# Joined sums of weighed states: VectorE's and TensorE's order at the join moved by one state

## The chip, the core and the metric

The kernel runs on one core of one Trainium2 chip. The metric is the device time in microseconds (us). Five engines work side by side, each with a queue of its own that it takes in order: TensorE (PE, matrix products and transposes), VectorE (DVE), ScalarE (ACT), GpSimd (POOL) and SyncE (SP, which here issues DMAs). They wait for each other by semaphores.

## What is computed

Two transformer-like layers over 2048 tokens of width 512. Layer 0 is a masked linear layer and a SwiGLU block with low-rank parts. Layer 1 is a selective state-space layer followed by a small mixture of experts. The change lies in the state-space layer, whose core is this recurrence over the tokens, for 1024 channels (`D_IN`) and 16 states (`N`):

```python
def step(state, inp):
    dt_t, B_t, C_t, u_t = inp
    dA = jnp.exp(dt_t[..., None] * A)
    state = state * dA + (dt_t * u_t)[..., None] * B_t[:, None, :]
    y = jnp.einsum('bdn,bn->bd', state, C_t)
    return (state, y)
```

So `y` is a sum over the 16 states, each weighed with its column of `C`. Around it stand the input projection, a convolution over four tokens, the projections that give `dt`, `B` and `C`, the gate, the output projection, a router and the experts.

## The kernel before, in words

Layer 1 takes the 2048 tokens in eight chunks of 256 (`NCH`, `CH`). In a chunk `i` the 1024 channels are two groups of 512 (`NDG`), and each group has 16 states: 32 steps `s`, written by hand as 32 slots in a loop of every engine (`iteration`). `st = s % 16` is the state in its group. Chunk `i`'s slots also carry work of the chunk before it (`p`: output projection, router, experts) and of the next one (`n`: input projection `x_tile`, `convolve`, `u`, `wx`, `dt_tile`, gates). The first chunk has no `p`, the last no `n`.

What one state costs, by engine:

- GpSimd makes `dbu` (`db`, L2097), dt times u times B, up to four states ahead of the scan.
- ScalarE writes the exponentials into `ps_a` (`exps`, L1757), in two halves, four instructions a state. There is one `ps_a`, so the half of state `s` waits for the scan of the same half of state `s - 1`. Between the halves it keeps the last column of the state before (`keep_state`, L1777).
- VectorE scans: `h` from `ps_a` and `dbu`, in two halves (`scans`, L2273). `h` is a ring of four states.
- The sum over the states is made with tokens on the partitions, so TensorE turns `h` (a transpose, eight passes, four for each of two halves `t` of the tokens) into the PSUM banks `ps_h`.

The states of a group are summed in two ways. For states 0 to 3 (`KC = 4`) GpSimd weighs `h` with `C` (`weigh_h`, L2131), and TensorE adds them up inside PSUM while it turns them (`add_h`, L1487; `init_acc`, L1475, puts in the term with D). After state 3 ScalarE copies that sum to `acc` in two halves: that is the join (`join_acc`, L1949, in the slot with `st == JOIN_AT`, 5, behind the exponentials of state 6 in its queue and ahead of those of state 7). For states 4 to 15 TensorE turns `h` unweighed (`turn_h`, L1502) and VectorE adds it to `acc` with its weight from `c_cur` (`add_state`, L2289, two instructions, one for each `t`).

`ps_h` has one bank for each `t`. So `turn_h` of state `s` waits, half by half, until state `s - 1` is added (for state 4: until its half is joined), and until state `s` is scanned. `add_state` waits for the turn of its half. The scan of state `s` waits for the turn of state `s - 4`, for `dbu` and for its half of `ps_a`.

The order at the join, before. VectorE: scan 5, scan 6, add 4, scan 7, add 5, add 6, scan 8, add 7, scan 9, add 8, and from there on one scan and one addition a slot. TensorE in the first group of a middle chunk: `add_h` of state 3, turn 4, a quarter of the output projection (q 5, L1526), turn 5, q 6, turn 6, `x_tile` 0, turn 7, q 7, `x_tile` 1, turn 8, `convolve` 0, `x_tile` 2, turn 9. In the second group: turn 4, `turn_tsb`, turn 5, the first part of the experts, turn 6, `dt_tile` 0 and 1, turn 7, turn 8, `dt_tile` 2 and 3, a second part of the experts, turn 9.

Other lines that the steps below touch: `make_u` (VectorE, L2303) reads the bank that `x_tile` and `convolve` of a tile wrote; `x_tile(m)` waits for `u` of tile `m - 3`, which had the same bank. `dt_add` (GpSimd, L2177) needs ScalarE's logarithm (`dt_log`, L1882) of the next chunk.

Of the kernel before, what the change touches and what calls it, by code (L numbers as in the profile page):

```python
# [42 lines left out]
NS = 16  # L43
# [40 lines left out]
JOIN_AT = 5  # L84
# [1026 lines left out]
def layer_1(nc, A, x2_dram, bt_dram, out, W, c, sb, ps, sems):  # L1111
# [229 lines left out]
    def _(pe):  # L1341
# [260 lines left out]
        def iteration(i, p, n, first, second):  # L1602
            for s in range(STEPS):
                st = s % NS
                if st == JOIN_AT + 1:
                    turn_h(i, s - 2)
                elif st == JOIN_AT + 2:
                    turn_h(i, s - 1)
                elif st > JOIN_AT + 2:
                    turn_h(i, s)  # L1610
                if first:
                    for m in GB_FIRST.get(s, ()):
# [24 lines left out]
                if s == FIRST_X:  # L1637
                    if n is not None:
                        x_tile(n, 0, False)
                    turn_h(i, s)  # L1640
                if p is not None and s:
                    for q in WO_AT.get(s, ()):
                        out_projection(p, q)
                        if q == 5:
                            turn_h(i, s - 1)
                if p is not None and s == RA_AT:
                    pe.wait_ge(S["t4_lo"], p * TT + TT)
                    router(p)
# [37 lines left out]
                    add_h(i, s - st + ADD_AT[st], first)  # L1686
                if st == 3:
                    init_acc(i, s // NS)
                if st == JOIN_AT + 1 and (p is None or s > NS):
                    turn_h(i, s - 1)  # L1690
                if p is not None and n is not None and s == NS + JOIN_AT + 1:
                    experts(p, 0)
                if st == JOIN_AT + 2 and s != FIRST_X:
                    turn_h(i, s)

        for m in range(3):
# [560 lines left out]
    def _(dve):  # L2257
# [147 lines left out]
        def iteration(i, p, n, first, second):  # L2405
            for s in range(STEPS):
                scans(i, s, first)
                st = s % NS
                if s == 0 and not first:
                    make_sg(i, 2)  # L2410
                if n is not None:
                    for m in at_slot(XT_AT, s, 4):
                        make_u(n, m)
                if s == JOIN_AT + 1:
                    dve.wait_ge(S["c_done"], i + 1)
                if st == JOIN_AT + 2:
                    add_state(i, s - 2)
                elif (st == 0 or st > JOIN_AT + 2) and not (first and s == 0):
                    add_state(i if s else i - 1, (s - 1) % STEPS)
                if p is not None:  # L2420
                    for m in at_slot(YB_AT, s):
                        make_y(p, m)
                if first and s == 2:
                    make_sg_first(2)
                    make_sg_first(3)
                if s == (3 if first else 2):
                    make_sg(i, 4)
                if p is not None and s == 4:
                    add_out_projection(p, 0)
                if s == 4:  # L2430
                    make_sg(i, 6)
                if p is not None and s == 8:
                    add_out_projection(p, 1)
                for m in at_slot(YA_AT, s):
                    make_y(i, m)
                if n is not None and s == WX_AT + 4:
                    make_sg(n, 0)
                if n is not None and s == WX_AT + 3:
                    mean_squares(n)
                if n is not None and s == WX_AT + 5:  # L2440
                    rms_apply(n)
                if p is not None and s == RA_AT + 3:
                    choose(p)
                if st == JOIN_AT + 1:
                    add_state(i, s - 2)
                if st == JOIN_AT + 2:
                    add_state(i, s - 1)

        nc.vector.memset(hist[:], 0.0).then_inc(S["begun"], 1)
# [99 lines left out]
```

## Time and profile before

| | us |
|---|---|
| time, median of 3 runs | 1513.37 (1512.45 to 1514.31) |
| time of the profiled execution | 1512.44 |
| its span, first to last instruction | 1510.3 |
| PE busy, share of the span | 1349.8, 89% |
| DVE busy | 1213.1, 80% |
| POOL busy | 1028.2, 68% |
| ACT busy | 952.1, 63% |
| L2273, the scans, x512 | 595.8, 1205 ns each |
| L2289, the additions, x384 | 267.9, 737 ns each |
| L1502, the turns, x1536 passes | 226.4, idle before them 65.3, of it 60.0 for L2289 |

Layer 1's scans begin at 530.5 us and end at 1476 us; layer 0 and the preparation of layer 1 lie before. In the rows below a time is the start of an instruction or of a run of like ones (x says how many), the next number how long it took, and brackets hold the idle time of the engine before it with what ended that. Matmuls overlap, so the distance from one start to the next is their cost, not the time in the row. PEclk is the share of full speed (2.4 GHz) that TensorE was granted.

### The profile page before, as it was taken

What the parts mean: (1) busy time and instruction counts of PE and PEld (TensorE: products, weight loads), DVE (VectorE), ACT (ScalarE), POOL (GpSimd) and SP (SyncE); (2) the same over time, 40 slices, a digit from 0 to 9 for tenths busy, and PEclk for the clock granted to TensorE, in tenths of its full rate; (3) what the DMA queues carried; (4) which work ended last, traced back from release to release, by engine and by line L of the source; (5) the groups of instructions that cost most, each with busy time, mean ns of one, the idle gap of its engine ahead of it and who ended that gap; (6) DMA issues with size and microseconds to landing.
All of it is one profiled execution on the core that took longest, in us unless ns stands there. A gap on an engine that the chain in (4) does not pass through costs nothing.

```text
span 1510.3 us, 25293 instructions
## 1 busy us (share of the span) xinstructions
PE 1349.8 (89%) x8817; PEld 1006.2 (67%) x8817; DVE 1213.1 (80%) x1643; ACT 952.1 (63%) x2617; POOL 1028.2 (68%) x697
## 2 busy tenths in 40 slices
PE   6899999999999959699899899899899999988677
PEld 5566677768776748568668667667766766855543
DVE  5794674556443469999999999999999999999994
ACT  3432343233321577788888897798798888886761
POOL 0353242313212398998998999899899899899870
PEclk9799999999999979899999999999999999999689
DMA  9531222101100200100110110020030020020001
GB/s 331 195 112 37 91 79 84 56 29 36 36 29 15 87 18 1 57 29 15 57 42 1 57 57 1 31 83 1 15 99 1 15 86 14 1 71 29 1 1 42
DMA packets 32388, 77.16 MB, mean 51 GB/s; under 512 B 3667, under 2 KB 4723, under 8 KB 31750
## 3 DMA queue, kind: packets, MB, share of 16 engines
q1 hardware_dynamic: 32262, 75.55, 15.1%
q8 instruction: 70, 1.15, 0.3%
q14 instruction: 56, 0.46, 0.1%
HBM read 66.99 MB, written 8.55 MB: 50 GB/s over the span
## 4 chain that ended last, share of the span: by engine, by line
PE 31%; POOL 13%; DVE 12%; ACT 6%; issue 5%; DVEq 0%; ACTq 0%; POOLq 0%
PE ps_h L1502 10%; DVE h L2273 7%; POOL h L2131 7%; POOL dbu L2097 6%; PE ps_m L1466 4%; DVE acc L2289 3%; ACT ps_a L1757 2%; PE ps_o L1526 2%; PE ps_m L165 2%; PE ps_s L1466 2%; PE ps_m L166 2%; PE ps_m L167 2%; PE ps_m L1426 2%; ACT ab L1889 1%; PE ps_s L165 1%
## 5 line engine op out<-in xcount | busy, mean ns | idle before, releaser
L2273 DVE TENSOR_TENSOR_SCAN h<-ps_a,dbu 128x512 f32<-128x512 f32 x512 | 595.8, 1205 | 21.3 <-ACT ps_a L1757 7.1
L2097 POOL TENSOR_TENSOR dbu<-dtu,b_all 128x1020 f32<-128x1020 f32 x256 | 598.3, 2358 | 14.4 <-DVE h L2273 13.9
L1757 ACT ACTIVATE ps_a<-dt,a_neg 128x256 f32<-128x256 f32 (+1 forms) x1024 | 442.9, 466 | 67.7 <-DVE h L2273 66.6
L1502 PE MATMUL ps_h<-ident,h 128*128 128x128 f32 x1536 | 226.4, 290 | 65.3 <-DVE acc L2289 60.0
L2289 DVE SCALAR_TENSOR_TENSOR acc<-ps_h,c_cur,acc 128x512 f32<-128x512 f32 x384 | 267.9, 737 | 16.9 <-PE ps_h L1502 16.3
L1502 PEld LDWEIGHTS ps_h<-ident,h 128*128 128x128 f32 x1536 | 183.1, 149 | 123.0 <-DVE h L2273 82.4
L724 POOL TENSOR_TENSOR hid_l<-hid,hid_h 128x256 f16<-128x256 f32 (+1 forms) x88 | 77.4, 883 | 155.0 <-ACT hid_h L610 154.8
L2131 POOL TENSOR_TENSOR h<-h,c_all 128x1024 f32<-128x1024 f32 x64 | 151.1, 2362 | 19.2 <-ACT carry L1777 19.2
L602 ACT ACTIVATE sil<-ps_gu 128x256 f32<-128x256 f32 (+1 forms) x88 | 33.9, 385 | 180.6 <-PE ps_gu L167 180.6
L165 PE MATMUL ps_m<-h_h,wi_h 128*128 128x256 f16 x432 | 119.4, 276 | 2.6 <-PEq L155 2.4
L166 PE MATMUL ps_m<-h_l,wi_h 128*128 128x256 f16 x432 | 119.2, 276 | 0.0
L167 PE MATMUL ps_m<-h_h,wi_l 128*128 128x256 f16 x432 | 119.2, 276 | 0.0
L1526 PE MATMUL ps_o<-wo,y 128*128 128x512 f32 x224 | 107.6, 603 | 7.7 <-DVE x L2391 7.7
L1487 PE MATMUL ps_h<-ident,h 128*128 128x128 f32 x512 | 70.4, 283 | 36.9 <-POOL h L2131 36.8
L165 PE MATMUL ps_gu<-h_h,g_h 128*128 128x256 f16 (+1 forms) x352 | 96.6, 274 | 3.8 <-DVE u_l L1016 2.9
L1487 PEld LDWEIGHTS ps_h<-ident,h 128*128 128x128 f32 x512 | 59.9, 145 | 56.0 <-POOL h L2131 43.7
L167 PE MATMUL ps_gu<-h_h,g_l 128*128 128x256 f16 (+1 forms) x352 | 96.5, 274 | 0.0
L166 PE MATMUL ps_gu<-h_l,g_h 128*128 128x256 f16 (+1 forms) x352 | 96.5, 274 | 0.0
L165 PE MATMUL ps_gu<-h_h,u_h 128*128 128x256 f16 (+1 forms) x352 | 96.1, 273 | 0.0
L166 PE MATMUL ps_gu<-h_l,u_h 128*128 128x256 f16 (+1 forms) x352 | 96.1, 273 | 0.0
L167 PE MATMUL ps_gu<-h_h,u_l 128*128 128x256 f16 (+1 forms) x352 | 96.1, 273 | 0.0
L732 POOL COPY x<-x 128x1024 f32<-128x1024 f32 x8 | 8.3, 1037 | 120.5 <-issue 120.5
(406 smaller groups left out, 2876.8 us busy)
## 6 DMA issues: line engine op xcount, KB each, us to landing
b_all<-bt_scratch SPq DMA_DIRECT2D x32, 512.0 KB, 3.9
wm<-in_wmod SPq DMA_DIRECT2D x7, 1024.0 KB, 5.2
wo<-in_wmod SPq DMA_DIRECT2D x5, 1024.0 KB, 8.6
xa<-in_x SPq DMA_DIRECT2D x8, 512.0 KB, 4.5
stage<-in_W_in SPq DMA_DIRECT2D x4, 1024.0 KB
x_scratch<-x SPq DMA_DIRECT2D x8, 512.0 KB, 3.1
c_all<-bt_scratch SPq DMA_DIRECT2D x8, 512.0 KB, 6.0
x<-x_scratch SPq DMA_DIRECT2D x8, 512.0 KB, 3.6
```

Of the source, the lines that this page charges most:

```text
L165: pe.matmul(out, lh, rh, start=(first and k == 0), stop=False)
L166: pe.matmul(out, lh, rl, start=False, stop=False)
L167: mm = pe.matmul(out, ll, rh, start=False, stop=(last and k == n - 1))
L1466: pe.matmul(x_bank(m, first), diag_t[:, m, tap], xw[:, m % 2, tap:tap + CH], start=(tap == 0), stop=False)
L1487: tr = pe.matmul(ps_h[:, t, j * P:(j + 1) * P], h[:, s % RING, j, t * P:(t + 1) * P], W["ident"][:], is_transpose=True, start=(begin and j ...
L1502: tr = pe.transpose(ps_h[:, t, j * P:(j + 1) * P], h[:, s % RING, j, t * P:(t + 1) * P], W["ident"][:])
L1526: mm = pe.matmul(ps_o[:], y[:, k, tok], W["wo"][:, k], start=(k == 0), stop=(k == KI - 1))
L1757: ex = nc.scalar.activation(ps_a[:, j, j % 2:], dt[:, m, j % 2:], ACT.Exp, scale=a_neg[:, m, st:st + 1])
L2097: nc.gpsimd.tensor_tensor(dbu[:, s % AHEAD, :, 1:], dtu[:, :, 1:], b_all[:, st, 1:].unsqueeze(1).to_broadcast([P, DG, CH - 1]), ALU.mult). ...
L2131: nc.gpsimd.tensor_tensor(h[:, s % RING], h[:, s % RING], c_all[:, s % NS, :].unsqueeze(1).to_broadcast([P, DG, CH]), ALU.mult).then_inc(S ...
L2273: nc.vector.tensor_tensor_scan(h[:, s % RING, two].rearrange("p j t -> p (j t)"), ps_a[:, two].rearrange("p j t -> p (j t)"), dbu[:, s % A ...
L2289: op = nc.vector.scalar_tensor_tensor(part, ps_h[:, t], c_t, part, ALU.mult, ALU.add)
```

## The change

VectorE adds state 4 one slot later, after the scan of state 7. To come level again it adds two states in the slots of states 7 and 8 (4 and 5, 6 and 7) where before it added one in the slot of state 6 and two in that of state 7. TensorE's turns move along: turn 5 goes to the head of slot 7, turn 6 behind `x_tile` 0 or to the end of slot 7, turn 7 to the head of slot 8 and turn 8 to its end. The scans, `dbu`, the exponentials, the join and all DMAs stay where they are.

The order after. VectorE: scan 6, scan 7, add 4, add 5, scan 8, add 6, add 7, scan 9, add 8. TensorE in the first group: turn 4, q 5, q 6, turn 5, `x_tile` 0, turn 6, q 7, `x_tile` 1, turn 7, `convolve` 0, `x_tile` 2, turn 8, turn 9. In the second group: turn 4, `turn_tsb`, the first part of the experts, turn 5, `dt_tile` 0 and 1, turn 6, turn 7, `dt_tile` 2 and 3, the second part of the experts, turn 8, turn 9.

```diff
@@ TensorE, iteration
                 if st == JOIN_AT + 1:
                     turn_h(i, s - 2)
                 elif st == JOIN_AT + 2:
+                    turn_h(i, s - 2)
+                elif st == JOIN_AT + 3:
                     turn_h(i, s - 1)
-                elif st > JOIN_AT + 2:
+                elif st > JOIN_AT + 3:
                     turn_h(i, s)
...
                 if s == FIRST_X:
                     if n is not None:
                         x_tile(n, 0, False)
-                    turn_h(i, s)
+                    turn_h(i, s - 1)
                 if p is not None and s:
                     for q in WO_AT.get(s, ()):
                         out_projection(p, q)
-                        if q == 5:
-                            turn_h(i, s - 1)
...
-                if st == JOIN_AT + 1 and (p is None or s > NS):
-                    turn_h(i, s - 1)
                 if p is not None and n is not None and s == NS + JOIN_AT + 1:
                     experts(p, 0)
                 if st == JOIN_AT + 2 and s != FIRST_X:
+                    turn_h(i, s - 1)
+                if st == JOIN_AT + 3:
                     turn_h(i, s)
@@ VectorE, iteration
                 if st == JOIN_AT + 2:
+                    add_state(i, s - 3)
+                elif st == JOIN_AT + 3:
                     add_state(i, s - 2)
-                elif (st == 0 or st > JOIN_AT + 2) and not (first and s == 0):
+                elif (st == 0 or st > JOIN_AT + 3) and not (first and s == 0):
                     add_state(i if s else i - 1, (s - 1) % STEPS)
...
-                if st == JOIN_AT + 1:
+                if st == JOIN_AT + 2:
                     add_state(i, s - 2)
-                if st == JOIN_AT + 2:
+                if st == JOIN_AT + 3:
                     add_state(i, s - 1)
```

## Rows read from the trace of the kernel before

**Rows 1.** Chain of waits: page's shares by engine, then two pieces.
```profile
PE 31%; POOL 13%; DVE 12%; ACT 6%; issue 5%; DVEq 0%; ACTq 0%; POOLq 0%
...
902.27 2.41 DVE h L2273 x2
...
1020.36 2.41 DVE h L2273 x2
```

**Rows 2.** Busy by stretch: us, PE, PEld, DVE, ACT, POOL, PEclk, DMA share, GB/s.
```profile
911.06:953.36 42.30, 42.30 (x286) 35.27 (x286) 40.74 (x52) 34.76 (x111) 35.69 (x23) 1.00 0.04 14
953.36:973.66 20.30, 16.75 (x140) 13.70 (x139) 19.34 (x32) 16.05 (x48) 20.13 (x11) 1.00 0.00 1
863.89:867.39 3.50, 3.50 (x20) 2.13 (x20) 3.50 (x5) 2.91 (x9) 3.34 (x8) 1.00 0.81 260
982.06:985.56 3.50, 3.50 (x14) 2.50 (x13) 3.50 (x5) 2.90 (x9) 3.34 (x8) 0.54 0.82 261
```

**Rows 3.** Timeline of DVE at the first join and after it.
```profile
911.77 1.41 DVE L2289 SCALAR_TENSOR_TENSOR acc<-ps_h,c_cur,acc 128x512 f32<-128x512 f32 x2 [1.06 <-PE ps_h L1502]
...
916.89 1.41 DVE L2289 SCALAR_TENSOR_TENSOR acc<-ps_h,c_cur,acc 128x512 f32<-128x512 f32 x2 [0.17 <-PE ps_h L1502]
...
928.35 0.42 DVE L2303 SCALAR_TENSOR_TENSOR u<-th,ps_m 128x256 f32<-128x256 f32 x1
```

**Rows 4.** Timeline of PE at the first join and after it.
```profile
911.04 1.06 PE L1502 MATMUL ps_h<-ident,h 128*128 128x128 f32 x8 [0.40 <-ACT acc L1949]
911.94 1.88 PE L1526 MATMUL ps_o<-wo,y 128*128 128x512 f32 x4
913.66 1.04 PE L1502 MATMUL ps_h<-ident,h 128*128 128x128 f32 x8
...
926.51 1.04 PE L1502 MATMUL ps_h<-ident,h 128*128 128x128 f32 x8
927.38 1.89 PE L1466 MATMUL ps_m<-xw,diag_t 128*128 128x256 f32 x8
...
929.22 0.27 PE L165 MATMUL ps_m<-h_h,wi_h 128*128 128x256 f16 x1
...
930.53 1.04 PE L1502 MATMUL ps_h<-ident,h 128*128 128x128 f32 x8
```

**Rows 5.** Timeline of ACT at the first join.
```profile
910.29 1.09 ACT L1949 ACTIVATE acc<-ps_h 128x512 f32<-128x512 f32 x2 [1.13 <-PE ps_h L1487]
...
911.74 0.89 ACT L1757 ACTIVATE ps_a<-dt,a_neg 128x256 f32<-128x256 f32 x2
```

**Rows 6.** Timeline of DVE at the second join and after it.
```profile
973.64 2.34 DVE L2273 TENSOR_TENSOR_SCAN h<-ps_a,dbu 128x512 f32<-128x512 f32 x2 [0.51 <-POOL dbu L2097]
...
981.01 1.38 DVE L2289 SCALAR_TENSOR_TENSOR acc<-ps_h,c_cur,acc 128x512 f32<-128x512 f32 x2
982.31 2.33 DVE L2273 TENSOR_TENSOR_SCAN h<-ps_a,dbu 128x512 f32<-128x512 f32 x2
```

**Rows 7.** Timeline of PE after the second join.
```profile
981.88 1.68 PE L1502 MATMUL ps_h<-ident,h 128*128 128x128 f32 x8 [2.15 <-DVE acc L2289]
983.35 1.91 PE L1426 MATMUL ps_m<-tsb,w_dt 128*128 128x256 f32 x4
...
986.92 1.04 PE L1502 MATMUL ps_h<-ident,h 128*128 128x128 f32 x8
```

**Rows 8.** Timelines of ACT and of POOL, later in the second group.
```profile
990.34 1.05 ACT L1882 ACTIVATE ab<-ab 128x1024 f32<-128x1024 f32 x1
...
984.61 6.98 POOL L2097 TENSOR_TENSOR dbu<-dtu,b_all 128x1020 f32<-128x1020 f32 x3
991.56 2.37 POOL L2177 TENSOR_TENSOR dt<-dt,ab 128x1024 f32<-128x1024 f32 x1
```

**Rows 9.** Timelines of POOL in the first and of DVE in the last chunk.
```profile
636.90 2.36 POOL L2177 TENSOR_TENSOR dt<-dt,ab 128x1024 f32<-128x1024 f32 x1 [3.20 <-ACT ab L1882]
...
1442.70 1.41 DVE L2289 SCALAR_TENSOR_TENSOR acc<-ps_h,c_cur,acc 128x512 f32<-128x512 f32 x2 [2.15 <-PE ps_h L1502]
```

## The prediction

> **What bounds the kernel now.** Layer 1 runs eight chunks of 256 tokens, and from the second to the seventh one repeats the other, so I worked on one chunk and multiplied. I read the chain of waits first: TensorE carries most of it, with GpSimd and VectorE behind; the chain passes the same two scans at 902.27 and at 1020.36, so a chunk takes 118.1 us, and this one (number 3, counted from 0) is the one I worked on [rows 1]. That is an average over stages, so I then took the busy times by stretch [rows 2]. In the 42.3 us from the turn of state 4 to the scan of state 16 TensorE is busy for all 42.30, VectorE for 40.74 and GpSimd for 35.69: TensorE sets the time. I call this stage B. In the 20.3 us after it GpSimd is busy for 20.13; this is stage C, and it ends with GpSimd's `dbu` for state 23. From there to the next chunk's state 3 VectorE is busy nearly without a break; I call it stage D. GpSimd in it has no idle time worth naming either: its row of three `dbu` ends at 991.59 and `dt_add` starts at 991.56, just after ScalarE's logarithm ended at 990.34 + 1.05 = 991.39 [rows 8].
>
> The change touches the joins, at slots 6 to 9 of each group of 16 states: the first lies at the head of stage B, the second at the head of stage D. The question is what it does to TensorE there in B, and to VectorE there in D.
>
> **Part 1: VectorE scans state 7 before it adds state 4.** No instruction is added or removed; each state has two scans (one pair takes 2.24 us from start to next start) and two additions (1.30). Before, VectorE waits 1.06 us for the turn of state 4, adds it at 911.77, and scans state 7 when the two additions are over, at 913.10 [rows 3]. The gap looks as if it could be filled with the scan. But that scan reads `ps_a`, whose exponentials ScalarE writes only after the two copies of the join (`join_acc` stands ahead of `exps(7)` in its queue): the copies run from 910.29, the exponentials of the first half from 911.74 for 0.89 us [rows 5]. So the scan can start near 912.72, only 0.4 us earlier than before, and state 4's addition moves from 911.77 to 912.72 + 2.24 = 914.96.
>
> **Part 2: who waits for that, in stage B.** Two latencies come from the rows: a turn's second half may start 0.87 us after the matching addition started (addition at 981.01, turn at 981.88), and an addition starts 0.73 us after its turn started (911.04, 911.77) [rows 3, 4, 6, 7]. A turn of eight passes takes 0.87 us from start to next start (926.51 to 927.38), a quarter of an output projection 1.72 (911.94 to 913.66), a convolution 1.84 (927.38 to 929.22), an `x_tile` 1.31 (929.22 to 930.53) [rows 4].
> - Turn 5 now stands behind both quarters: TensorE is there at 911.94 + 3.44 = 915.38. Its halves may go at 914.96 + 0.87 = 915.83 and 915.61 + 0.87 = 916.48, so it ends at 916.92 instead of 916.25: 0.67 us lost. The 0.15 that turn 6 lost before (the 0.17 wait of addition 6 [rows 3]) is saved: +0.5.
> - Turns 6, 7 and 8 have tile work between them. Turns 8 and 9 now stand with nothing between: turn 9 needs state 8 added, which needs turn 8. The first half goes 0.70 + 0.87 after turn 8's start, the second 0.65 later, and 0.44 more ends it: 2.66 us for what took 1.74. +0.9.
> - VectorE comes out later than TensorE: by the same steps it scans state 10 from 928.16 to 930.40, and `u` of tile 0, at 928.35 before [rows 3], comes at 930.40 and is done near 930.9. `x_tile(3)` writes over the bank that it reads, and TensorE is there at 930.66: +0.25. The same for the next two tiles costs some 0.15 together.
>
> Stage B: 0.5 + 0.9 + 0.4 = 1.8 us a chunk. TensorE has no idle time in it to take this up, and stage C starts from its end. From both sides: 1.0 if ScalarE lets the scan go earlier and `u` is in time, 2.4 if each wait is 0.1 to 0.2 dearer.
>
> **Part 3: stage D.** Here VectorE is the one without slack. State 23's scan waits for `dbu` until 973.64 [rows 6]. Before, state 20's addition filled the time ahead of that wait; now it stands behind it. So one addition (1.30 us) falls onto the busy stretch. Additions 5 and 7 each wait 0.24 for their turns, the 0.16 wait of addition 6 goes: 1.6 us, and state 25 is scanned near 983.9 instead of 982.31 [rows 6].
>
> Then the moved turn 8: before it was the first thing of its slot, at 981.88. Now it stands behind turn 7, two `dt` tiles and a part of the experts. In chunk 3 TensorE's granted clock is 0.54 there, so half of the 3.5 us or more at 1.2 GHz, in chunk 2 it is 1.00 [rows 2]. At the low clock that work took from 983.35 to turn 9 at 986.92 before, 3.6 us [rows 7]; turn 7 now ends where turn 8 did, so turn 8 starts at 986.92 and addition 8 at 987.65, where VectorE would be ready at 983.87 + 2.24 = 986.11: 1.5 more, 3.1 in all. At full clock turn 8 starts near 985.4 and nobody waits. Chunks 1, 3 and 6 have the low clock there, three of six.
>
> Does it reach the end? GpSimd would have 1.2 us of slack at the weighing of state 1, but at `dt_add` it has 0.1 [rows 8], and ScalarE's logarithm hangs on VectorE's scans through the exponentials ahead of it in its queue. So 1.5 (full clock) or 2.9 (low clock) passes on. Bounds: 0.3 and 3.2.
>
> Of the clock the Trainium skill (TensorE: Matmul & The Clock Gate, Part 1) says that "the default state is throttled, and activity releases the throttle". By that rule the longer waits of TensorE at the head of stage D would give the low clock in all six chunks and not in three; the trace has it at like waits both ways, so I keep three.
>
> **The two ends.** In the first chunk there is no output projection between the turns; by the same steps I take 1.2 for B and 1.5 for D (there GpSimd waits 3.20 us for the logarithm, so all passes on [rows 9]): 2.7. The last chunk has no tiles of a next one. There VectorE waits 2.15 us at the second join [rows 9], and the scan does fill part of it: one addition more behind, 1.30, less some 0.9 gained twice, and waits of 0.2 to 0.3 for turns: 0.8, between -0.8 and 1.6. Semaphores, DMAs and the other queues (SP, GpSimd's order) are not moved.
>
> **The sum.** 6 x 1.8 = 10.8 for B, 3 x 1.5 + 3 x 2.9 = 13.2 for D, 2.7 and 0.8: +27.5 us. The profiled execution took 1512.4 (span 1510.3 and 2.1 around it) and would take 1539.9; the median of the runs is 0.9 above it, so 1540.9.
>
> **The rivals.**
> 1. Stage D's loss is taken up by slack (GpSimd's 1.2 us, ScalarE overtaking): D gives 0.3 a chunk and B stays: 10.8 + 1.8 + 2.7 + 0.8 = 16, so 1529. For it: GpSimd's slack at the weighing. Against: the 0.1 at `dt_add`.
> 2. The low clock in all six chunks, and longer: 3 x 1.4 = 4.2 more and some, 1546. The page's rule above speaks for it.
> 3. Faster: the filled gap counts and the new waits don't. The scan of state 8 comes 0.4 us earlier (917.8 where the additions of state 6, at 916.89, end at 918.2 [rows 3]), twice in each of seven chunks, and some 0.8 twice in the last: 14 x 0.4 + 1.6 = 7, so 1506. This decides if TensorE had slack of over 1.5 us at turn 9 and VectorE more than an addition's worth in D. Against: TensorE busy 42.30 of 42.30.
> 4. The order doesn't matter, since all engines are level at the end of each stage: 1513.
>
> **How the numbers follow.** My forecast has 0.52, rival 1 0.20, rival 2 0.16, rival 3 0.07, rival 4 0.05. A difference of 0.2%, 3 us, is about what a measurement of this kernel can tell. Faster 0.08, same 0.04, slower 0.88. For the range: B between 1.0 and 2.4, D between 0.3 and 3.2, six times, are 8 to 34 us, with the ends 10 to 38; I take 1524 to 1550, which leaves out rivals 3 and 4 and a little on top.
>
> **What would show it.** In the changed profile: scan 7 starts right behind ScalarE's exponentials and not in the 1.06 us gap; TensorE's idle time before turns (waiting for the additions) appears in stage B, at turn 5 and turn 9, where it had none; the period of the middle chunks is 121.5 to 123 instead of 118.2; VectorE waits for turn 8 at the second join where TensorE's clock is low; `dt_add` on GpSimd waits for ScalarE. It is wrong if the period is under 119.5, if turn 9 doesn't wait, or if GpSimd starts the next chunk's weighing on time.

## The result and the profile after

The changed kernel takes 1546.0 us (median of 6 runs, 1540.75 to 1550.43); the kernel before, run beside it, takes 1512.43 (6 runs, 1510.95 to 1514.31). The ratio is 1.0213, 95% interval 1.0195 to 1.0231: slower by 33.6 us, where +27.5 was forecast (1540.9, range 1524 to 1550). The profiled execution is the lowest of the six, 1540.75, with a span of 1538.6. The stages below come from it, so they have to add up to 28.3 us of span, not to 33.6.

First the page of the kernel after: the chain's shares, and the groups of scans, turns and additions.

```profile
PE 25%; POOL 19%; DVE 12%; issue 7%; ACT 6%; DVEq 0%; POOLq 0%; ACTq 0%
...
L2273 DVE TENSOR_TENSOR_SCAN h<-ps_a,dbu 128x512 f32<-128x512 f32 x512 | 596.4, 1207 | 50.3 <-ACT carry L1777 21.9
...
L1502 PE MATMUL ps_h<-ident,h 128*128 128x128 f32 x1536 | 230.7, 293 | 85.4 <-DVE acc L2289 79.7
L2289 DVE SCALAR_TENSOR_TENSOR acc<-ps_h,c_cur,acc 128x512 f32<-128x512 f32 x384 | 268.7, 740 | 18.0 <-PE ps_h L1502 17.3
```

The work is the same (596.4 us of scans for 595.8, 268.7 of additions for 267.9). What grew is idle time: TensorE waits 79.7 us for additions before its turns, where it waited 60.0. The chain has lost TensorE (31% to 25%) and won GpSimd (13% to 19%), which by itself tells neither where nor why.

So I cut each chunk into stages, at instructions close to the prediction's bounds. Stage B runs from the start of the first join (`acc`, L1949; the prediction began 0.75 us later, at turn 4) to GpSimd's weighing of state 16, C from there to the scan of state 23, D from there to `dt_add` (the prediction let it run on to the next chunk's state 3), and the rest of the chunk is the remainder. From the starts in the timelines, in us:

| chunk | B before | B after | D before | D after | period before | period after |
|---|---|---|---|---|---|---|
| 1 | 42.97 | 44.61 | 17.82 | 20.49 | 118.40 | 122.30 |
| 2 | 42.97 | 44.61 | 17.87 | 20.63 | 118.17 | 122.47 |
| 3 | 42.98 | 44.61 | 17.92 | 20.12 | 118.13 | 121.95 |
| 4 | 42.97 | 44.61 | 17.81 | 19.39 | 118.17 | 121.24 |
| 5 | 42.97 | 44.61 | 17.94 | 20.55 | 118.17 | 122.39 |
| 6 | 42.97 | 44.61 | 17.83 | 20.66 | 118.20 | 122.87 |

C and the remainder are the same within 0.4. The six periods grew by 24.0 us, the first chunk by 3.6 (B 2.0, D 1.6), the last by 1.3, what follows its last addition by 1.6, and what lies ahead of the first chunk's join took 2.2 less: 28.3.

**Stage B.** VectorE at the first join of chunk 3 of the kernel after (start, duration, engine, line; in brackets the idle time before):

```profile
922.39 2.34 DVE L2273 TENSOR_TENSOR_SCAN h<-ps_a,dbu 128x512 f32<-128x512 f32 x2 [1.76 <-ACT carry L1777]
924.65 1.39 DVE L2289 SCALAR_TENSOR_TENSOR acc<-ps_h,c_cur,acc 128x512 f32<-128x512 f32 x2
926.19 1.41 DVE L2289 SCALAR_TENSOR_TENSOR acc<-ps_h,c_cur,acc 128x512 f32<-128x512 f32 x2 [0.15 <-PE ps_h L1502]
...
932.43 1.41 DVE L2289 SCALAR_TENSOR_TENSOR acc<-ps_h,c_cur,acc 128x512 f32<-128x512 f32 x2 [0.68 <-PE ps_h L1502]
933.76 2.33 DVE L2273 TENSOR_TENSOR_SCAN h<-ps_a,dbu 128x512 f32<-128x512 f32 x2
936.46 1.41 DVE L2289 SCALAR_TENSOR_TENSOR acc<-ps_h,c_cur,acc 128x512 f32<-128x512 f32 x2 [0.37 <-PE ps_h L1502]
937.78 2.33 DVE L2273 TENSOR_TENSOR_SCAN h<-ps_a,dbu 128x512 f32<-128x512 f32 x2
940.03 0.40 DVE L2303 SCALAR_TENSOR_TENSOR u<-th,ps_m 128x256 f32<-128x256 f32 x1
```

and ScalarE ahead of the scan of state 7:

```profile
919.93 1.09 ACT L1949 ACTIVATE acc<-ps_h 128x512 f32<-128x512 f32 x2 [0.84 <-PE ps_h L1487]
...
921.38 0.89 ACT L1757 ACTIVATE ps_a<-dt,a_neg 128x256 f32<-128x256 f32 x2
```

The gap of 1.06 us [rows 3] isn't filled but has grown: the scan now waits 1.76 us, until 922.39, just behind the exponentials of its first half (921.38 + 0.89 = 922.27), as in [rows 5]. (The trace puts this wait down to `carry`, L1777, the one that came last by the profile.) TensorE in the same stretch (the group x8 is a turn; L165 here is the first product of `x_tile` 3):

```profile
920.67 1.06 PE L1502 MATMUL ps_h<-ident,h 128*128 128x128 f32 x8 [0.40 <-DVE h L2273]
921.58 3.60 PE L1526 MATMUL ps_o<-wo,y 128*128 128x512 f32 x8
925.52 1.23 PE L1502 MATMUL ps_h<-ident,h 128*128 128x128 f32 x8 [0.35 <-DVE acc L2289]
...
935.82 1.04 PE L1502 MATMUL ps_h<-ident,h 128*128 128x128 f32 x8
937.35 1.22 PE L1502 MATMUL ps_h<-ident,h 128*128 128x128 f32 x8 [0.50 <-DVE acc L2289]
938.41 1.89 PE L1466 MATMUL ps_m<-xw,diag_t 128*128 128x256 f32 x8
940.14 0.27 PE L1467 MATMUL ps_m<-sel,rows 128*128 128x256 f16 x1
940.48 0.28 PE L165 MATMUL ps_m<-h_h,wi_h 128*128 128x256 f16 x1
```

From turn 4 to turn 10 TensorE took 911.04 to 930.53 = 19.49 us before [rows 4], and 920.67 to 941.80 = 21.13 now. Those 1.64 us are all of what B lost, and they lie at three places. From turn 4 to the end of turn 6, without `x_tile` 0, 6.23 us became 6.78 (turn 5 waits and runs slowly): 0.55. Turns 8 and 9, which took 0.87 each, now take 938.41 - 935.82 = 2.59 together for 1.74: 0.85. `x_tile` 3 starts 0.34 behind the instruction before it, where 0.11 is the rule [rows 4]: 0.23.

**Stage D.** VectorE, TensorE and GpSimd at the second join of chunk 3:

```profile
984.91 2.34 DVE L2273 TENSOR_TENSOR_SCAN h<-ps_a,dbu 128x512 f32<-128x512 f32 x2 [1.90 <-POOL dbu L2097]
987.16 1.39 DVE L2289 SCALAR_TENSOR_TENSOR acc<-ps_h,c_cur,acc 128x512 f32<-128x512 f32 x2
989.16 1.60 DVE L2289 SCALAR_TENSOR_TENSOR acc<-ps_h,c_cur,acc 128x512 f32<-128x512 f32 x2 [0.61 <-PE ps_h L1502]
```

```profile
988.04 1.94 PE L1502 MATMUL ps_h<-ident,h 128*128 128x128 f32 x8 [2.98 <-DVE acc L2289]
989.77 1.91 PE L1426 MATMUL ps_m<-tsb,w_dt 128*128 128x256 f32 x4
991.48 1.92 PE L1502 MATMUL ps_h<-ident,h 128*128 128x128 f32 x8
```

```profile
995.88 6.99 POOL L2097 TENSOR_TENSOR dbu<-dtu,b_all 128x1020 f32<-128x1020 f32 x3
1005.03 2.36 POOL L2177 TENSOR_TENSOR dt<-dt,ab 128x1024 f32<-128x1024 f32 x1 [2.16 <-ACT ab L1882]
```

The wait for `dbu` is 1.90 us for 0.51 [rows 6]: nothing stands ahead of it now, and state 20 is added behind it. GpSimd, which had no gap at `dt_add` [rows 8], waits 2.16 us there for ScalarE's logarithm. Turns 5 and 6 take 1.94 and 1.92 us here, for 1.22 and 1.04 in chunk 2: that is the granted clock. The busy times by stretch, PEclk behind the five busy times; the stretches start 2.2 us and 8.2 us behind the scan of state 23, chunks 2, 3 and 4:

```profile
864.65:870.65 6.00, 2.96 (x20) 2.42 (x20) 5.84 (x9) 5.41 (x17) 5.77 (x7) 1.00 0.29 102
870.65:876.15 5.50, 5.46 (x24) 3.78 (x25) 4.30 (x5) 2.94 (x9) 5.34 (x9) 0.69 0.50 182
987.11:993.11 6.00, 5.07 (x20) 4.51 (x20) 5.29 (x8) 4.87 (x15) 5.76 (x7) 0.50 0.29 112
993.11:998.61 5.50, 4.75 (x29) 3.19 (x27) 5.27 (x7) 3.26 (x10) 5.34 (x9) 0.92 0.48 172
1109.05:1115.05 6.00, 2.96 (x20) 2.42 (x20) 5.84 (x9) 5.41 (x17) 5.77 (x7) 1.00 0.37 104
1115.05:1120.55 5.50, 4.82 (x30) 3.49 (x31) 5.35 (x7) 3.34 (x10) 5.34 (x9) 1.00 0.61 177
```

Chunk 4 has the full clock throughout and the shortest D, 19.39. Chunk 3 has 0.50 at turns 5 and 6 (D 20.12); chunks 1, 2, 5 and 6 have 0.69 to 0.70 in the later stretch, ahead of turn 8 (D 20.49 to 20.66). There VectorE waits for turn 8, in chunk 2:

```profile
876.34 1.41 DVE L2289 SCALAR_TENSOR_TENSOR acc<-ps_h,c_cur,acc 128x512 f32<-128x512 f32 x2 [0.93 <-PE ps_h L1502]
```

So D lost 6 x 1.58 = 9.5 us without the clock (chunk 4: 19.39 - 17.81), less 0.3 for the spread of before, and 5.5 us over 19.39 in five chunks.

### The profile page after: what moved, and what is told of

It reads as the page before. It is cut to its first block, busy times and chain, and to the rows that moved or that the text cites. A ratio compares the mean times of both kernels' runs of the same rounds, so it can differ in the third digit from the quotient of the medians.

```text
span 1538.6 us, 25293 instructions
## 1 busy us (share of the span) xinstructions
PE 1357.0 (88%) x8817; PEld 1004.0 (65%) x8817; DVE 1213.8 (79%) x1643; ACT 953.7 (62%) x2617; POOL 1027.3 (67%) x697
## 4 chain that ended last, share of the span: by engine, by line
PE 25%; POOL 19%; DVE 12%; issue 7%; ACT 6%; DVEq 0%; POOLq 0%; ACTq 0%
POOL dbu L2097 10%; PE ps_h L1502 8%; POOL h L2131 8%; DVE h L2273 7%; PE ps_m L1466 3%; DVE acc L2289 3%; ACT ps_a L1757 2%; PE ps_s L1466 2%; PE ps_m L165 2%; PE ps_m L166 2%; PE ps_m L167 2%; PE ps_o L1526 1%; PE ps_m L1426 1%; POOL dtu L2203 1%; POOL rms L2169 1%
## 5 line engine op out<-in xcount | busy, mean ns | idle before, releaser
L2273 DVE TENSOR_TENSOR_SCAN h<-ps_a,dbu 128x512 f32<-128x512 f32 x512 | 596.4, 1207 | 50.3 <-ACT carry L1777 21.9
L1502 PE MATMUL ps_h<-ident,h 128*128 128x128 f32 x1536 | 230.7, 293 | 85.4 <-DVE acc L2289 79.7
L2289 DVE SCALAR_TENSOR_TENSOR acc<-ps_h,c_cur,acc 128x512 f32<-128x512 f32 x384 | 268.7, 740 | 18.0 <-PE ps_h L1502 17.3
L165 PE MATMUL ps_m<-h_h,wi_h 128*128 128x256 f16 x432 | 119.6, 277 | 3.1 <-PEq L155 2.4
L1487 PE MATMUL ps_h<-ident,h 128*128 128x128 f32 x512 | 69.3, 280 | 36.1 <-POOL h L2131 36.1
L165 PE MATMUL ps_gu<-h_h,g_h 128*128 128x256 f16 (+1 forms) x352 | 96.0, 273 | 1.8 <-DVE u_l L1016 1.2
L165 PE MATMUL ps_gu<-h_h,u_h 128*128 128x256 f16 (+1 forms) x352 | 95.9, 273 | 0.0
```

The costliest lines, as they stand in the source:

```text
L165: pe.matmul(out, lh, rh, start=(first and k == 0), stop=False)
L1487: tr = pe.matmul(ps_h[:, t, j * P:(j + 1) * P], h[:, s % RING, j, t * P:(t + 1) * P], W["ident"][:], is_transpose=True, start=(begin and j ...
L1502: tr = pe.transpose(ps_h[:, t, j * P:(j + 1) * P], h[:, s % RING, j, t * P:(t + 1) * P], W["ident"][:])
L2273: nc.vector.tensor_tensor_scan(h[:, s % RING, two].rearrange("p j t -> p (j t)"), ps_a[:, two].rearrange("p j t -> p (j t)"), dbu[:, s % A ...
L2289: op = nc.vector.scalar_tensor_tensor(part, ps_h[:, t], c_t, part, ALU.mult, ALU.add)
```

## The experiments

My theory: B and D each lose by themselves, B by the late turns 5 and 9 and late `u`, D by the addition that fell behind the wait for `dbu`, with the low clock on top. A ratio is to the kernel before, measured beside it, with its 95% interval. B and D are those of the middle chunks of the profiled execution.

**One join alone.** Both sides, TensorE and VectorE, of the change in one group of states only. The first join (in the second one `late = 0`; VectorE's first place, against the kernel before, the other places are left out):

```diff
-                if st == JOIN_AT + 2:
+                late = 1 if s // NS == 0 else 0
+                if late and st == JOIN_AT + 2:
+                    add_state(i, s - 3)
+                elif st == JOIN_AT + 2 + late:
                     add_state(i, s - 2)
```

> The change at the first join of each chunk (slots 6 to 9) alone; the second join keeps its old order. My theory: the two joins lose time separately. Stage B (first join to the weighing of state 16) is 1.6 us longer in each middle chunk, as in the changed kernel's trace (44.61 for 42.97), stage D (scan of state 23 to dt_add) stays at 17.9. Sum with the first chunk about +12 us, a time near 1524.5. Rival: stage D is longer because VectorE comes out of stage B late; then D lengthens here too, and the time is 1535 or more.

Measured: 1526.01 (4 runs), 1.0089 [1.0072, 1.0106]; B 44.61, D 17.8 to 18.0. As expected: B loses its 1.63 alone, and D nothing.

The second join (`late = 1 if s // NS == 1 else 0`):

> The change at the second join (slots 22 to 25) alone. My theory: stage B stays at 42.97, stage D goes from 17.9 to 19.5 where TensorE's clock is full and to 20.5 where it is low near turns 5 to 8; sum +17 to +21 us, a time near 1531, with a wider spread between executions than before (which had 3.4 us). Rival (slack takes up the loss): D at most 0.5 longer, a time under 1518.

Measured: 1522.75 (4 runs), 1.0071 [1.0054, 1.0088]; B 42.98 to 42.99, D 20.74 in chunk 1 and 19.39 in the five others. The place is right, but the size is under what I expected, because the low clock came ahead of turn 8 in one chunk of six. The busy times by stretch for chunks 1 and 3 (PEclk 0.85 and 1.00):

```profile
739.81:751.31 11.50, 8.43 (x43) 6.01 (x44) 10.14 (x13) 8.47 (x25) 11.10 (x15) 0.85 0.49 139
980.38:991.88 11.50, 7.80 (x51) 5.93 (x51) 11.19 (x15) 8.76 (x26) 11.10 (x15) 1.00 0.49 141
```

The two together are 13.6 + 10.3 = 23.9 us of the 33.6. I find no third cause in the order of the work: B and D have the same values as in the whole change wherever the clock is full. Of the 9.7 us that are left, the traces show 4.15 as the low clock behind the second join (5.5 us in five chunks of the whole change, 1.35 in one here). Another 5.3 is how far the median of the whole change lies above its profiled execution, and no trace shows what that is.

**One engine alone.** VectorE's new order with TensorE's old one (against the kernel after; the first of TensorE's places, the others go back in the same way):

```diff
@@ TensorE, iteration
                 if st == JOIN_AT + 1:
                     turn_h(i, s - 2)
                 elif st == JOIN_AT + 2:
-                    turn_h(i, s - 2)
-                elif st == JOIN_AT + 3:
                     turn_h(i, s - 1)
```

> VectorE's new order with TensorE's old one. My theory: what costs in stage D is VectorE's own addition behind the wait for dbu (+1.57, the same in all chunks, since turn 8 stands ahead of the dt tiles again and the clock can't reach VectorE), so D is 19.4 to 19.5 in every chunk. In stage B turn 5 waits ahead of q 6 and turn 8 for an addition behind the out projection's: B about +3. Sum near +31 us, a time near 1543. Rival (TensorE's moved turns are what costs): B and D near the old values, a time under 1520.

Measured: 1555.52 (4 runs), 1.029 [1.0273, 1.0307]; B 46.4 to 47.8, D 20.0 to 21.0. That is slower than I said, in both stages. The old turn 5 waits for the late addition of state 4 (2.07 us at the first join, 4.29 at the second) and holds up what follows it, q 6 at the first join; VectorE then waits for that projection:

```profile
938.41 0.69 DVE L2391 SCALAR_TENSOR_TENSOR x<-ps_o,x 128x512 f32<-128x512 f32 x1 [2.93 <-PE ps_o L1526]
```

I had said that the clock couldn't reach VectorE at the second join in this order. It did: the granted clock was low in all six chunks around or behind the wait for turn 5, and D is 20.0 to 20.2 in four chunks and 21.0 in the two where it stayed low for more than 8 us behind the scan of state 23. There is no chunk with the full clock, so this run doesn't show what the order alone costs in D. B is 46.4 in three chunks and 47.6 to 47.8 in the three where the clock was low at the first join too.

TensorE's new order with VectorE's old one (against the kernel after, the first of two places):

```diff
@@ VectorE, iteration
-                if st == JOIN_AT + 2:
-                    add_state(i, s - 3)
-                elif st == JOIN_AT + 3:
+                if st == JOIN_AT + 2:
                     add_state(i, s - 2)
```

> TensorE's new order with VectorE's old one. My theory: turn 9 right behind turn 8 costs 0.9 and the wait of x_tile 3 for u 0.3: B +1.3. In stage D turn 6 now stands behind dt tiles 0 and 1, which wait for ScalarE's copy until about 3.8 us after the scan of state 23, so addition 6 comes 1.5 late: D +1.6, more where the clock is low. Sum +18 to +24, a time near 1534. Rival (VectorE's order alone is what costs): a time within 3 us of before.

Measured: 1533.26 (4 runs), 1.0133 [1.0116, 1.015]; B 44.52 to 44.53, D 19.38 to 19.40 in all six. As expected, with B 0.25 us a chunk above what I said. Late turns cost nearly as much in B as the whole change, late additions alone more: that turns move along with the additions is the cheaper way to do it, not a cure. With VectorE's old order, state 20 is added ahead of the wait for `dbu`, and D still is 19.4, since the addition of state 22 now waits 1.72 us for turn 6. That turn starts at 987.94, behind `dt` tiles 0 and 1, for which TensorE waited 2.75 us for ScalarE, as I had expected:

```profile
983.22 2.34 DVE L2273 TENSOR_TENSOR_SCAN h<-ps_a,dbu 128x512 f32<-128x512 f32 x2 [0.51 <-POOL dbu L2097]
988.58 1.41 DVE L2289 SCALAR_TENSOR_TENSOR acc<-ps_h,c_cur,acc 128x512 f32<-128x512 f32 x2 [1.72 <-PE ps_h L1502]
```

```profile
986.97 1.13 PE L1426 MATMUL ps_m<-tsb,w_dt 128*128 128x256 f32 x4 [2.75 <-ACT tsb L1904]
987.94 1.04 PE L1502 MATMUL ps_h<-ident,h 128*128 128x128 f32 x8
```

So D's 1.58 us come from VectorE's moved addition in the whole change and from TensorE's moved turn 6 here. Taking back VectorE's order alone doesn't win them back.

**Is turn 9 a term of its own?** In the kernel after, turn 8 goes ahead of `x_tile` 2 at the first join, so that a tile lies between turns 8 and 9:

```diff
+                if s == JOIN_AT + 3:
+                    turn_h(i, s)
                 if n is not None:
                     for m in XT_AT.get(s, ()):
...
-                if st == JOIN_AT + 3:
+                if s == NS + JOIN_AT + 3:
                     turn_h(i, s)
```

> The whole change, but at the first join turn 8 stands ahead of x_tile 2 and no longer right ahead of turn 9. My theory: the wait between turns 8 and 9 (0.9 by my sum, 1.5 start to start for 0.87 of work) is then covered by the tile, and addition 8 and u follow earlier; a wait of about 0.3 stays. Stage B of the middle chunks 43.6 to 43.8 for 44.61, stage D as in the changed kernel, a time 5 to 7 us below it, near 1540. Rival (the loss in B is turn 5's wait and VectorE's lateness, whatever stands between 8 and 9): B within 0.2 of 44.61.

Measured: 1543.54 (4 runs), 1.0195 [1.0167, 1.0223]; B 44.64. The rival holds: no gain. TensorE at the same place (turn 9, the convolution, the instruction ahead of `x_tile` 3, its first product):

```profile
939.95 1.22 PE L1502 MATMUL ps_h<-ident,h 128*128 128x128 f32 x8
941.00 1.89 PE L1466 MATMUL ps_m<-xw,diag_t 128*128 128x256 f32 x8
942.74 0.27 PE L1467 MATMUL ps_m<-sel,rows 128*128 128x256 f16 x1
943.30 0.28 PE L165 MATMUL ps_m<-h_h,wi_h 128*128 128x256 f16 x1 [0.29 <-DVE u L2305]
```

Turn 9 still starts 0.2 late and runs 0.2 slowly, `x_tile` 3 now waits 0.45 more than the rule where it waited 0.23, and tiles 4 and 5 wait 0.14 each, which they didn't. From turn 4 to turn 10 it takes 20.88 for 21.13, and the two later waits give that back.

Then turn 7 ahead of `x_tile` 1 as well, which takes away the 0.68 us that VectorE waits for it (turn 7's old place at the head of slot 8 goes at this join; not shown):

```diff
@@ as above, and
+                if s == FIRST_X and n is not None:
+                    turn_h(i, s)
                 if s == JOIN_AT + 3:
                     turn_h(i, s)
```

> The whole change with turn 7 ahead of x_tile 1 and turn 8 ahead of x_tile 2 at the first join. The run with turn 8 alone moved left stage B at 44.64, and VectorE's u still late for x_tile 3; so the theory is now that B is longer by VectorE's lateness (1.7 us at the scan of state 10), which reaches TensorE through u, and not by the wait between turns 8 and 9. Then taking away VectorE's wait of 0.7 us for turn 7 must shorten B although TensorE's queue has the same work: B 44.1 to 44.3. Rival (TensorE's waits at its turns set it): B stays at 44.6.

Measured: 1537.44 (4 runs), 1.0143 [1.0116, 1.017]; B 43.86, under what I expected. The addition of state 7 waits no more:

```profile
934.91 1.41 DVE L2294 SCALAR_TENSOR_TENSOR acc<-ps_h,c_cur,acc 128x512 f32<-128x512 f32 x2
```

and turn 4 to turn 10 takes 20.37. Of the 1.64 us, 0.75 are won back once VectorE has less to wait for. So about half of B's loss depended on VectorE being late, and it reaches TensorE either at turn 9 or at `x_tile` 3 to 5.

**Does VectorE's amount of work set B?** In the kernel after, VectorE waits 0.37 us ahead of 936.46 and hardly at all from there until B ends, so it could be VectorE that sets it. I made the additions of states 11 and 12 of the first group lighter by half, in the kernel after and in the kernel before (the sum lacks the other half of these two states):

```diff
-                op = nc.vector.scalar_tensor_tensor(part, ps_h[:, t], c_t, part, ALU.mult, ALU.add)
+                w = DG * P // 2 if s in (11, 12) else DG * P
+                op = nc.vector.scalar_tensor_tensor(part[:, 0:w], ps_h[:, t, 0:w], c_t, part[:, 0:w], ALU.mult, ALU.add)
```

> The kernel after, in which VectorE adds states 11 and 12 of each chunk with half of their columns only (the other half of the two weighed states is missing from the sum): about 0.28 us less for each of four additions, 1.1 us of VectorE's work less in stage B; TensorE's work stays. Asked: what sets stage B in the changed kernel, VectorE's work or TensorE's order. The kernel after has VectorE busy 26.54 of 26.82 us behind scan 10, without a gap of its own at the scans, and TensorE busy 26.76 of 26.82. Theory VectorE: B falls from 44.61 by 0.7 to 1.1, to 43.5 to 43.9; seven chunks, 6 us, near 1540. Rival TensorE (u, x_tile and turns come one after another by TensorE's own order): B stays 44.4 to 44.65, and the time within 2 us of the kernel after.

Measured: 1542.37 (4 runs), 1.0198 [1.0177, 1.0219]; B 44.61 in all six. The time is 3.6 us below the kernel after, more than the 2 that the rival allowed, but the ratios' intervals overlap and B didn't move.

> The kernel before with the same lighter additions of states 11 and 12 (half of their columns missing). My prediction held that TensorE alone sets stage B there (busy 42.30 of 42.30); then B stays at 42.9 to 43.0 and the time at that of the kernel before, within 0.2%. If VectorE sets it as much, B falls by 0.3 to 1.1, and the time by 2 to 7 us. Earlier runs took 1.7 and 3.4 us of TensorE's work from B and got 0.0 and 0.1 for it; so I now expect that B falls a little, 0.1 to 0.5, until TensorE holds it.

Measured: 1513.75 (10 runs), 0.9999 [0.9984, 1.0015]; B 42.97 to 42.98; it didn't fall by the 0.1 to 0.5 that I expected. In both kernels VectorE's load alone doesn't set B: TensorE's queue is full beside it and holds the stage at its length. The 1.1 us of VectorE became waits, mostly for ScalarE, as here in the light kernel after:

```profile
957.44 2.34 DVE L2273 TENSOR_TENSOR_SCAN h<-ps_a,dbu 128x512 f32<-128x512 f32 x2 [0.42 <-ACT carry L1777]
960.02 0.42 DVE L2304 SCALAR_TENSOR_TENSOR u<-th,ps_m 128x256 f32<-128x256 f32 x1 [0.24 <-ACT th L1842]
```

An engine without gaps need not be the one that sets the time, or not alone.

**Does TensorE's amount of work set B?** In the kernel before, a quarter of the output projection goes ahead of the join, where TensorE waits 1.16 us for GpSimd:

```diff
-WO_AT = {0: (1,), 1: (2,), 3: (3,), 4: (4,), 6: (5, 6), 7: (7,)}
+WO_AT = {0: (1,), 1: (2,), 3: (3,), 4: (4,), 6: (6,), 7: (7,)}
...
+                    if p is not None:
+                        out_projection(p, 5)
                     add_h(i, KC - 1, first)
...
-                        if q == 5:
+                        if q == 6:
                             turn_h(i, s - 1)
```

> The kernel before (no part of the change), but quarter 5 of the output projection stands ahead of add_h of state 3, in TensorE's wait for GpSimd, instead of behind turn 4. If TensorE's queue sets stage B, as I say, 1.72 us of work leave it and the join comes at most 0.4 later: B 41.6 to 42.0 for 42.97 and a time near 1505. Rival (stage B is bound by VectorE too, busy 40.7 of 42.3): B at most 0.4 shorter, a time of 1509 or more.

Measured: 1516.99 (8 runs), 1.0026 [1.0008, 1.0043]; B 42.98. TensorE at the join, turns 5 and 6:

```profile
911.39 1.04 PE L1502 MATMUL ps_h<-ident,h 128*128 128x128 f32 x8
913.94 1.22 PE L1502 MATMUL ps_h<-ident,h 128*128 128x128 f32 x8 [1.52 <-DVE acc L2291]
```

The 1.72 us saved are a wait of 1.52 for the addition of state 5: turn 6 starts 913.94 - 908.77 = 5.17 behind turn 4, where it started 916.25 - 911.04 = 5.21 behind it. Up to turn 6 the chain of join, turn 4, addition 4, scan 7, addition 5 is as long as TensorE's work. The rival came out, not the B of 41.6 to 42.0 that I expected. Moving q 7 ahead of turn 6 as well (`6: (6, 7)`):

> The kernel before, with quarter 5 of the output projection ahead of add_h of state 3 and quarter 7 ahead of turn 6 (behind turn 5 and quarter 6). With quarter 5 alone moved, stage B kept its 42.98, because turn 6 waits for VectorE's addition of state 5: TensorE then waited 1.5 us there. If B is the way to turn 6 over VectorE plus TensorE's work behind turn 6, quarter 7 in that wait takes 1.5 to 1.7 us off that work: B 41.5 to 42.0, the join 0.4 later, a period of 117.1 to 117.6 for 118.2 and a time near 1508. Rival (VectorE's own pace from state 10 on, with u waiting for ScalarE's tanh, binds as soon as TensorE has slack): B 42.8 or more, a time of 1513 or more.

Measured: 1518.0 (12 runs), 1.0013 [1.0001, 1.0025]; B 42.86. Again the rival came out, and it says more than the run before: behind turn 6, too, 1.72 us of TensorE's work less win only 0.12. From turn 6 to turn 13 TensorE takes 945.29 - 918.63 = 26.66, where it took 943.03 - 916.25 = 26.78 with a quarter of a projection more:

```profile
918.63 1.19 PE L1502 MATMUL ps_h<-ident,h 128*128 128x128 f32 x8
...
945.29 1.04 PE L1502 MATMUL ps_h<-ident,h 128*128 128x128 f32 x8
```

From the addition of state 4 on VectorE has hardly a gap; besides 0.16 us at turn 6 the one of note is `u` waiting for ScalarE's `th`:

```profile
934.88 0.42 DVE L2305 SCALAR_TENSOR_TENSOR u<-th,ps_m 128x256 f32<-128x256 f32 x1 [0.17 <-ACT th L1844]
```

So in the kernel before two chains lie side by side through the whole of stage B, within some 0.1 us of each other: TensorE's queue, and VectorE's with ScalarE's work for it. Lightening either one alone wins nothing; I have not lightened both. Neither version is faster than the kernel before; in chunk 3 the period is 0.3 and 0.2 us longer, since the join comes later behind `dt_add`.

**Stage D: the order or the clock?** In the kernel after, turn 8 right behind turn 7 at the second join (its old place at the end of slot 8 then stays for the first join only; not shown):

```diff
                 elif st == JOIN_AT + 3:
                     turn_h(i, s - 1)
+                    if s > NS:
+                        turn_h(i, s)
```

> The whole change, but at the second join turn 8 stands right behind turn 7, ahead of dt tiles 2 and 3 and the experts. My theory: where the clock is low in that work (chunks 1, 2, 5 and 6 of the changed kernel) VectorE no longer waits for it, so D is 19.4 to 19.6 there instead of 20.5; where it is low at turns 5 to 7, D is still 20.1. B 44.61. A time near 1539. Rival (the low clock costs at the turns themselves, not by what stands ahead of turn 8): D keeps its values up to 20.7 and the time its 1546.

Measured: 1542.42 (4 runs), 1.0203 [1.018, 1.0226]; D 19.38 to 20.04. The clock is low in the later stretch in four chunks (0.69 each), and that now costs 0, 0.4, 0.4 and 0.6 us and not 1.1 to 1.3, so the rest was turn 8's place. One chunk has it early, in the stretch of turns 5 and 6 (0.72), and pays 0.65 for it. D fell as expected; the time didn't clearly fall (the intervals of the two ratios overlap).

Then the kernel after with 16 more matmuls a chunk, 9 and 7, at the second join, where TensorE waits; nobody reads what they write (`fill(p, n, bank, times)` issues `times` products of 128x512 f16 into a bank of `ps_m`):

```diff
+                if p is not None and n is not None and s == NS + JOIN_AT + 2:
+                    fill(p, n, 0, 9)
+                if p is not None and n is not None and s == NS + JOIN_AT + 3:
+                    fill(p, n, 1, 7)
```

> The whole change, with 9 matmuls of 128x512 f16 that nothing reads in TensorE's wait ahead of turn 5 and 7 in that ahead of turn 7, second join, chunks 1 to 6 (about 0.22 us each, so 2.0 and 1.5 us of waits of 3.0 and 2.3). My theory: the spread and the part of the loss above 3.1 us a chunk come from the granted clock of 0.5 that follows these waits; filled, the clock stays at 1.0 from turn 5 to turn 9, D is 19.4 in all middle chunks, and the time near 1537 with a spread of under 4 us. Rival (the low clock comes and goes for other reasons): low stretches as often as before, 1546 and a spread near 10.

Measured: 1536.77 (4 runs, 1535.38 to 1540.5), 1.0164 [1.0136, 1.0192]; D 19.40 in five of six chunks, 19.83 in one. Chunk 3, with a granted clock of 1.00:

```profile
988.33:999.83 11.50, 9.31 (x58) 6.58 (x58) 11.19 (x15) 8.79 (x26) 11.10 (x15) 1.00 0.49 141
```

TensorE's added work does nothing but fill its waits, and what D had over 19.4 is gone in five chunks; in all six the clock is full from turn 5 to turn 9. The sixth (chunk 5) had the low clock earlier, at turn 4 and the experts behind it. Its turn 5 stood behind the late experts and the added matmuls, and VectorE waited for it:

```profile
1232.93 1.41 DVE L2298 SCALAR_TENSOR_TENSOR acc<-ps_h,c_cur,acc 128x512 f32<-128x512 f32 x2 [0.58 <-PE ps_h L1502]
```

One trace of each kernel would not settle this, since the second join alone had the low clock there in only one chunk of six without any added matmul. But all four runs (1535.38 to 1540.5) lie below all six of the kernel after (1540.75 to 1550.43), and the intervals of the ratios don't meet. So what D had over 19.4 was the clock. The 1.58 us are left: they are the order's.

## Why the prediction was right, and where it wasn't

**Sign and place.** Both stages that I named lost, and nothing else did by much. The profile shows what the prediction asked for: scan 7 right behind ScalarE's exponentials, waits before turns 5 and 9, periods of 121.2 to 122.9, `dt_add` waiting for ScalarE. Shifted by the 9.64 us between the two joins of chunk 3, scan 7, scan 10 and `u` come at 912.75, 928.14 and 930.39, where the prediction had put 912.72, 928.16 and 930.40.

**How far the sum's fit is luck.** For the six middle chunks it had 24.0 us, and 24.0 were measured. Its parts were not that good: B 10.8 for 9.8 measured, D 13.2 for 14.7, and C and the remainder, which it left out, 0.5 less than before. Misses of 1 to 1.5 us cancelled.

**Part 2, stage B.** Forecast 1.8 a chunk, measured 1.64, and step by step: turn 5 0.5 for 0.55, turn 9 0.9 for 0.85, `u` 0.4 for 0.23 (0.25 for `x_tile` 3 was right, the 0.15 for the next two tiles didn't come). What the sum got wrong is that it treated them as three causes. They are one lateness seen at three places: with turn 9's wait mostly taken away it came back at `x_tile` 3, 4 and 5. The sum holds for this order, but its terms are no list of what can be won back singly.

**"TensorE sets the time", from busy 42.30 of 42.30.** This was half the truth. Lighter work for VectorE changed nothing, so VectorE doesn't set it alone. But 1.72 us of TensorE's work less ahead of turn 6 won nothing, because a chain of the same length (5.17 and 5.21) stood beside it, and 1.72 us less behind turn 6 won 0.12, because VectorE's way is nearly as long there too. I took a full engine for the only limit. The forecast for B came out near all the same; the change delays VectorE too (the scan of state 10 came 17.85 us behind the join and not 15.62).

**Part 3, stage D.** The addition that falls behind the `dbu` wait: 1.5 forecast at full clock, 1.58 measured (chunk 4). It passed to GpSimd, as the 0.1 us of slack at `dt_add` said. Rival 1 (slack takes it up) and rivals 3 and 4 are out: no chunk shows a D under 19.39.

**The clock.** This is the term that was mis-sized. I took three chunks of six at 1.4 us more, by the places where the kernel before had it, 4.2 us in all; in the profiled execution there were five, at 0.73 to 1.27 more, 5.5 us. Two things were wrong in the step. The places don't carry over, since TensorE's waits are others now. And the low clock ahead of turn 8, which I costed, is one case; at turns 5 and 6, which I didn't, it costs 0.7. The median came out at rival 2's number (six chunks, 1546). That doesn't prove rival 2: the one execution with a trace has five chunks and 1540.75, and the others have no trace. Of this the Trainium skill (TensorE: Matmul & The Clock Gate, Part 1) says that activity releases the throttle; the matmuls that nobody reads are a test of that, and they agree (1.00 from turn 5 to turn 9 in all six chunks, where it was 0.50 at turns 5 and 6 of chunk 3). The rule doesn't say which chunk has it: with the same order at the second join it was one of six in one kernel and five of six in another.

**The ends.** The first chunk lost 3.6, not 2.7, nearly all of the miss in B (2.0 for 1.2). One pair of executions can't size this: with the old order at the first join, B of the first chunk took 42.3 to 43.2 in four kernels, with the new one 43.9 to 45.2 in four, so the loss is there and its size open. The last lost 1.3 for 0.8. What follows the last addition took 1.6 us more, and what lies ahead of the first join 2.2 less. The first of these isn't the order's: over the kernels here it took 30.0 to 33.8 us without a pattern by edit.

**The median against the profiled execution.** The forecast was made against one execution, and the median lies 5.3 us above the one that was profiled. The six executions had mean granted clocks of 0.948 to 0.956, and the two longest (1550.43 and 1548.78) had the two lowest, 0.948 and 0.949; the kernel with the added matmuls had 0.957 to 0.960 and 1535.4 to 1540.5. That could point to the clock for the spread as well. Other kernels speak against so simple a rule: with turns 7 and 8 moved, the run of 1533.07 us had the lowest mean clock of its four, 0.949, and of the runs with the added matmuls the longest, 1540.5, had the highest, 0.960. What the 5.3 us are stays open, since only one execution of each kernel has a trace.

No version here beats the kernel before.

## What to carry to other kernels

A gap ahead of an instruction is no free slot for another one until you have looked at what that other one waits for. Here the scan needed exponentials that stood in ScalarE's queue behind the very thing that made the gap, so the gap wasn't filled but grew to 1.76 us, and the addition that had stood in it came late: that cost 1.64 us at the first join and 1.58 at the second.

Where two engines hand work to and fro, go through each queue with the start-to-start latencies of the rows; that gave stage B's loss to 0.2 us and the start of `u`, 20 us behind the join, to 0.01. Don't read the terms as separate causes, and ask for each engine that is busy throughout whether a chain of the same length runs beside it: here two did, and lightening either one alone won 0.1 us at most.

## What the runs showed of the hardware

The granted clock of TensorE went to half in stretches of some 3 to 7 us in or just behind waits of 2 to 3 us (in chunk 3 of the kernel after, 0.50 around turn 5, which had waited 2.98 us), and a turn then took 1.92 us instead of 1.04. What it cost depended on where it fell. Behind the second join of the kernel after it was 0.7 us in the chunk that had it at turns 5 and 6, and 1.1 to 1.3 in the four that had it ahead of turn 8. In the kernel before it was 0 to 0.1, since nobody waited for that work (D 17.92 in chunk 3 with 0.54, 17.87 in chunk 2 with 1.00 [rows 2]). The same instructions in the same order had it in some chunks of an execution and not in others. Sixteen short matmuls without a purpose in each middle chunk kept it away from turns 5 to 9 in all six, and the median was 9.2 us lower (by the ratios, 1.0213 and 1.0164, 7.4 us), in a kernel that waits.
